# Shifted-window attention block: the queries' tiles widened from 98 to 128 columns, so that each scores matmul loads 128 columns

## What is computed

```python
xl = _ln(transpose(x, (0, 2, 3, 1)), norm1_w, norm1_b)
xl = roll(xl, shift=(-3, -3), axis=(1, 2))
xw = xl cut into 7 x 7 windows                      # 1024 windows of 49 tokens, 192 channels
q, k, v = split(einsum('bnc,oc->bno', xw, qkv_w) + qkv_b)
attn = softmax(einsum('bnhd,bmhd->bhnm', q, k) * dh ** -0.5)
out = einsum('bhnm,bmhd->bnhd', attn, v)
out = einsum('bnc,oc->bno', out, proj_w) + proj_b
xl = roll(windows put back, shift=(3, 3), axis=(1, 2))
xl = _ln(xl, norm2_w, norm2_b)
h = gelu(einsum('bhwc,oc->bhwo', xl, fc1_w) + fc1_b)
return transpose(einsum('bhwo,co->bhwc', h, fc2_w) + fc2_b, (0, 3, 1, 2)) + x
```

## Time and profile before

| | before |
|---|---|
| median of 3 runs | 3171.6 us (3171.49 to 3172.69) |
| time of the profiled execution | 3172.68 us |
| its span, first to last instruction | 3170.9 us |
| mean granted TensorE clock | 0.996 of full speed |
| TensorE matmul (PE) busy | 3136.1 us, 99% |
| TensorE weight load (PEld) busy | 3049.5 us, 96% |
| ScalarE (ACT) busy | 2976.5 us, 94% |
| VectorE (DVE) busy | 2500.6 us, 79% |
| GpSimd (POOL) busy | 1019.4 us, 32% |

### The profile page before, as it was taken

How to read it: one execution, slowest core, us unless ns; L and a number is a source line. 1 busy time by engine, 2 the same in 40 slices (tenths; PEclk the granted TensorE clock), 3 DMA queues, 4 the chain that set the end, 5 groups by cost and what they waited for, 6 DMA issues and landing times.

```text
span 3170.9 us, 76849 instructions
## 1 busy us (share of the span) xinstructions
PE 3136.1 (99%) x28076; PEld 3049.5 (96%) x28076; DVE 2500.6 (79%) x7210; ACT 2976.5 (94%) x5498; POOL 1019.4 (32%) x1292
## 2 busy tenths in 40 slices
PE   6999999999999999999999999999999999999998
PEld 6999999999999999999999999999999999999998
DVE  6787788778877887888788778877887788788876
ACT  3999999999999999999999999999999999999997
POOL 1333333333333333333333333333333333333332
PEclk8999999999999999999999999999999999999999
DMA  3112111111211121112111211121121112111211
GB/s 68 30 40 46 38 40 43 43 38 40 43 42 38 40 46 39 38 40 46 38 39 40 46 38 40 42 44 38 40 43 42 38 40 44 42 38 40 46 30 28
DMA packets 458709, 129.30 MB, mean 41 GB/s; under 512 B 392803, under 2 KB 458084, under 8 KB 458340
## 3 DMA queue, kind: packets, MB, share of 16 engines
q1 hardware_dynamic: 455012, 122.71, 18.3%
q10 hardware_dynamic: 3328, 1.68, 0.2%
HBM read 47.20 MB, written 38.54 MB: 27 GB/s over the span
## 4 chain that ended last, share of the span: by engine, by line
PE 98%; DVE 1%; SPq 1%; ACT 0%; issue 0%; POOL 0%; DMA 0%; POOLq 0%; DVEq 0%; ACTq 0%
PE psum L581 8%; PE psum L311 7%; PE psum L313 6%; PE psum L312 6%; PE psum L314 6%; PE psum L315 6%; PE psum L560 6%; PE psum L551 4%; PE psum L540 4%; PE psum L541 4%; PE psum L542 4%; PE psum L552 4%; PE psum L566 4%; PE psum L510 4%; PE psum L321 3%; PE psum L325 3%
## 5 line engine op out<-in xcount | busy, mean ns | idle before, releaser
L1116 POOL TENSOR_TENSOR ve<-mv,eps 98x4 f32<-98x4 f32 x256 | 133.1, 520 | 1821.4 <-DVE mv L916 1821.4
L921 DVE TENSOR_SCALAR xn<-psum,mv,rs 98x192 f32<-98x192 f32 x1024 | 460.9, 472 | 37.8 <-POOL rs L1118 33.6
L727 ACT ACTIVATE hh<-psum,b 128x392 fp32r<-128x392 f32 x768 | 452.6, 590 | 30.8 <-PE psum L552 6.4
L944 DVE TENSOR_TENSOR x_l<-psum,x_h 128x392 fp32r<-128x392 f32 x256 | 140.7, 550 | 396.5 <-ACT x_h L693 396.5
L730 ACT ACTIVATE hf<-psum,b 128x392 f32<-128x392 f32 x768 | 438.0, 589 | 3.1
L910 DVE BATCH_NORM_STATS2 st<-psum 98x6 f32<-98x192 f32 x1024 | 325.7, 349 | 102.6 <-PE psum L487 101.3
L1130 POOL TENSOR_TENSOR pr<-pr,rc 98x294 f32<-98x294 f32 x512 | 372.6, 737 | 56.4 <-DVE rc L991 56.4
L955 DVE TENSOR_TENSOR hl<-hf,hh 128x392 fp32r<-128x392 f32 x640 | 361.9, 566 | 8.3 <-ACT hf L730 8.1
L727 ACT ACT_TABLE_LOAD x253 | 324.6, 1283 | 4.5
L739 ACT ACT_TABLE_LOAD x252 | 323.3, 1283 | 4.5
L311 PE MATMUL psum<-x_h,w_mh 128*128 128x392 f32 x768 | 294.8, 384 | 1.7 <-ACT hf L730 1.2
(11 more groups left out here) (136 smaller groups left out, 10139.7 us busy)
## 6 DMA issues: line engine op xcount, KB each, us to landing
vbd<-vs SPq DMA_DIRECT2D x1024, 36.8 KB
xt<-in_x SPq DMA_DIRECT2D x112, 194.5 KB, 2.7
out<-xt SPq DMA_DIRECT2D x112, 194.5 KB, 2.0
xt<-in_x SPq DMA_DIRECT2D x112, 97.2 KB, 2.4
out<-xt SPq DMA_DIRECT2D x112, 97.2 KB, 2.1
xt<-in_x SPq DMA_DIRECT2D x112, 48.2 KB, 2.2
xt<-in_x SPq DMA_DIRECT2D x256, 0.8 KB, 2.0
xt<-in_x SPq DMA_DIRECT2D x128, 1.5 KB, 2.2
```

Source lines behind the costliest of these rows:

```text
L727: nc.scalar.activation(hh[:, m % HB, :], bank("fc1", m)[:, 0:T], ACT.Gelu, bias=b1[:, m:m + 1]).then_inc(s_hh, 1)
L921: nc.vector.tensor_scalar(xn[ln][:, j // 2, j % 2 * C:j % 2 * C + C], ln_chunk(("ln1", "ln2")[ln], j), mv[ln][:, j, 0:1], rs[ln][:, j:j + ...
```

## The change

The two tiles of queries get 128 columns for each window or pair in place of 98. The added 30 columns are zeroed by the same memsets as the rest and never written again. The scores matmuls load all 128 columns, and so write 128 partitions of the PSUM bank; partitions 98 to 127 get zeros that nobody reads. The keys, the moving operand, stay at 98 columns. ScalarE's views of the queries take the first 98 columns. No instruction is added, removed or moved: each engine has the same instructions in the same order.

```diff
-        qm = sb("qm", [128, NW, TP])
+        qm = sb("qm", [128, NW, 128])
         km = sb("km", [128, NW, TP])
-        qr = sb("qr", [128, PAIRS, TP])
+        qr = sb("qr", [128, PAIRS, 128])
         kr = sb("kr", [128, PAIRS, TP])
...
             def scores(u, j):
                 claim(u, [("s", j)], (s_qkv, QK_COPIES, QK_COPIES - 1))
-                ps = bank("s", j)[0:TP, :]
+
+                ps = bank("s", j)
                 for wi in range(2):
                     w = 2 * j + wi
                     nc.tensor.matmul(ps[:, TP * wi:TP * wi + TP], qm[:, w, :], km[:, w, :], start=True, stop=True)
...
-            q_side = qm.rearrange("p w (s n) -> p w s n", s=2)
+            q_side = qm[:, :, 0:TP].rearrange("p w (s n) -> p w s n", s=2)
             k_side = km.rearrange("p w (s n) -> p w s n", s=2)
-            q_side_r = qr.rearrange("p j (s n) -> p j s n", s=2)
+            q_side_r = qr[:, :, 0:TP].rearrange("p j (s n) -> p j s n", s=2)
```

## The result

| | before | after |
|---|---|---|
| median of 3 runs | 3171.6 us | 3238.3 us (3237.63 to 3239.48) |
| ratio, 95% interval | | 1.021 (1.019 to 1.023) |
| time of the profiled execution | 3172.68 us | 3237.63 us |
| its span | 3170.9 us | 3235.8 us |
| granted TensorE clock | 0.996 | 0.996 |

The account below looks back on a forecast made before the run. TensorE's matmul stream, busy 99% of the span, was taken as the bound, with scores bound by weight loads. 23 passes x 25 ns = 0.575 us a step, x 128 units = 73.6 us, gave 3246 us; range 3228 to 3256.

Parts of the forecast that it names:

- The bound: Scores matmuls on TensorE: the weight load, 86 ns for 98 columns, sets the pace, against 84 ns for the moving columns.
- The price: Each scores pass: 30 more columns loaded cost 25 ns, chosen from four readings of 20 to 26 ns.
- the two bias loads: Loads of two bias-product passes with 128 stationary columns: 0.30 us together, about 110 ns each, giving 110 - 86 = 24 ns.
- How many pay: Of a step's 24 scores passes, 11 in the first group and 12 in the second pay: 0.575 us a step.
- The free one: First load of the first scores group: beside line 315's matmul it has 170 ns, so a 110 ns load costs nothing.
- The sum: Whole kernel: 128 units x 0.575 us = 73.6 us, with the median going from 3171.6 to 3246 us, 2.3%.
- The term of 1 us for the first steps' lower clock: First steps, partly at the lower clock: the price of a few dozen passes doubles, some 1 us.
- What was put at nothing: Line 581's and line 311's loads behind the groups, ScalarE's query writes and VectorE's later scores: no cost, no newly exposed wait.
- Faster through a fast load: Rival for the scores loads: 128 columns load faster, passes take 84 ns, gaining 6 to 9 us: 3164 us; 4 in 100.
- The prediction's doubt: Scores loads: two passes for one float32 matmul might let them get Fast Weight Load; the time would be 3164 us.
- No change through a hidden load: Rival for the scores: moving columns set the pace and hide a load of 128; 3172 us stays; 5 in 100.
- The 155 ns of the bias products: Rival: scores passes cost as lines 474 and 475's do, 155 ns each, adding 212 us: 3384 us; 1 in 100.

## Why the prediction was right

**The bound.** That the load and not the moving columns sets the scores' pace was read from the bias products, since the scores' own rows couldn't tell 86 from 84 ns. Halving the moving columns shows it: 87 and 112 ns, as before.

**The price.** 25 ns a pass was taken from readings between 20 and 26. It is 111.7 - 86.7 = 25.0. The nearest row, the two bias loads, was right in type and width and 1 ns low by rounding; that the figure chosen is right to the tenth is luck. The Trainium skill ("TensorE: Matmul & The Clock Gate", LDWEIGHTS) gives a load as its columns divided by 1.2 GHz, the same 25 ns for 30 columns, and these runs agree with it on that slope; the distances are 5 ns above it.

**How many pay.** 11 in the first group and 12 in the second: 275 and 300 ns. The free one shows in the distance from the first pass to the second, 83 ns at both widths.

**The sum.** It was 8 us too high, for the most part in one step: "The stretch of 100 to 3000 us then shows that nothing is left over: matmuls are busy for all 2900 us." PE at 100% does not mean that TensorE never waits. It waited 68 ns a step ahead of line 321, 8.7 us over 128 units, and the longer scores filled that pause. 73.6 - 8.7 = 64.9 us, and a rest of 11 ns a step spread over many places, 1.4 us, make 66.3; 66.7 were measured between the medians and 64.9 between the two traces' spans. The 68 ns are read from start times. In the times themselves the runs with the variance earlier bear out 4.6 us of the 8.7, the difference between their 71.3 us and 66.7. Between these two kernels, without the wait, 73.6 - 71.3 = 2.3 us are missing as well, and what takes them is open. The term of 1 us for the first steps' lower clock was not there at all: the first unit's 24 passes do run at a granted clock of 0.50, but take only 0.52 us longer, and at the third unit's first scores, 78.5 us into the span, the changed kernel is just 0.08 us behind.

**What was put at nothing.** Line 582 took 2.00 us as before, ScalarE 2976.9 us for 2976.5. That VectorE gets its scores later exposed no new wait; it did the opposite. VectorE's chain moved back by 0.13 us and TensorE's arrival at line 321 by all 0.575, because both groups of scores sit between that chain's start and its consumer. With 64 columns it was the other way round, 0.13 us for VectorE and nothing for TensorE, and the wait grew.

**The rivals.** Faster through a fast load: the loads got longer, not shorter, and 112 columns lie on the line between 98 and 128, so it did not occur in float32. In bfloat16 it does, at 128 columns. The Trainium skill ("TensorE: Matmul & The Clock Gate", Weight-path perf modes) puts both conditions, 128 columns and a type other than float32, and these runs agree with it on both: records of 192 ns in float32 and 97 in bfloat16 at 128 columns, 124 in bfloat16 at 98. The prediction's doubt, that the split of a float32 matmul in two passes might count as another type, is answered: it doesn't. No change through a hidden load: excluded by the halved keys. The 155 ns of the bias products: not seen in the scores, whose passes don't change their number of rows.

## What to carry to other kernels

Padding a stationary operand to 128 columns can pay only where the type gets the fast load, and even in bfloat16 no gain in time could be told here; in plain float32 each column costs 0.83 ns as soon as the load is longer than the moving columns' time, so compare the two for every small matmul, by a row where one of them is nearly absent. A PE that is busy at 100% can still wait: compare the distance between starts with that of like neighbours, and expect such waits to swallow part of a slowdown, and part of a gain to run into them. When a stretch gets longer or shorter, ask on which side of another engine's chain it lies: delaying that chain's start by 0.13 us cost 15 us where its consumer didn't move with it. Before two operations are exchanged on an engine, look up all readers of both results, the nearest one in time first.

## What was not expected of the hardware

A bfloat16 load of 98 columns, without the fast way, is also quicker than a float32 one: in the run with 98 columns passes come 42 to 47 ns apart, so the load takes no more than that, where the line that fits float32 would give 87. Line 510's transposes of float32 are quicker, too, with load records that grow by 0.45 ns a column.

Fast loads seem not to overlap with what runs before them: with 128 bfloat16 columns the first load of the first group starts 0.17 us late in each step,

```profile
1609.63 0.11 PEld L562 LDWEIGHTS psum<-km,qm 128*128 128x128 bf16 x2 [0.17 <-issue]
```

and the one with 98 columns doesn't. Whether it is the fast load itself that waits for the array to be empty was not tried apart.

At a change between matmuls of 64 output columns and wider ones the next load starts late: 0.26 us behind the start of line 315's matmul in the run with 64 columns, where it started together with it before. That costs some 0.17 us at the second group's first passes. Two such changes next to passes of 392 columns cost 0.30 us a step together, about as much as they had on the scores' inner side, 0.31.
